# A routed two-layer feed-forward: the second layer's bias leaves TensorE for GpSimd, and its result alternates between two PSUM banks

## What is computed

```
t = to_tokens(x)                                # 2048 tokens x 192
gate_scores = ln(t) @ gate_w + gate_b           # 2048 x 6
topk_scores, topk_idx = top_k(gate_scores, 2)
topk_weights = softmax(topk_scores, axis=1)
hmid = gelu(einsum('nh,ehf->nef', ln(t), w1) + b1)    # 768 wide
expert_out = einsum('nef,efh->neh', hmid, w2) + b2    # 192 wide
sel = take_along_axis(expert_out, topk_idx[:, :, None], axis=1)
out = t + einsum('nk,nkh->nh', topk_weights, sel)
```

## Time and profile before

| what | value |
| --- | --- |
| three timed runs | 419.43, 415.05, 419.24 us; median 419.24 us |
| span of the profiled execution | 416.4 us; the page gives no other time of its own for it |
| TensorE busy | 349.8 us, 84% of the span |
| TensorE weight loads busy | 299.6 us, 72% |
| VectorE busy | 243.6 us, 59% |
| ScalarE busy | 182.3 us, 44% |
| GpSimd busy | 133.4 us, 32% |
| mean granted TensorE clock | 0.907 of 2.4 GHz |

### The profile page before, as it was taken

The page is one execution under the profiler, slowest core; times in us unless marked ns, Lnnn a source line. Parts: engine busy times, 40 slices in busy tenths (PEclk is TensorE's granted clock), DMA queues, the critical chain, the costliest instruction groups (busy, mean ns, idle before and its releaser), DMA issues.

```text
span 416.4 us, 10239 instructions
## 1 busy us (share of the span) xinstructions
PE 349.8 (84%) x2780; PEld 299.6 (72%) x2781; DVE 243.6 (59%) x961; ACT 182.3 (44%) x447; POOL 133.4 (32%) x163
## 2 busy tenths in 40 slices
PE   2668989889898889873089999999999999999625
PEld 0136877777777778662079999999999999999512
DVE  4443677777777777555235655555555656555246
ACT  1325767666666645430114434434344443444213
POOL 0000657766676773234101111122111221112100
PEclk9888999999999999955559999999999999999855
DMA  6422433323333310001301111111111111110066
GB/s 184 128 58 83 126 88 113 97 95 95 95 95 95 104 39 19 21 19 38 107 21 29 49 34 41 44 37 44 34 38 47 30 40 45 29 48 20 12 234 220
DMA packets 28053, 29.09 MB, mean 70 GB/s; under 512 B 5498, under 2 KB 24325, under 8 KB 28033
## 3 DMA queue, kind: packets, MB, share of 16 engines
q1 hardware_dynamic: 22498, 21.17, 17.9%
q0 software_dynamic: 3312, 6.33, 4.5%
q10 hardware_dynamic: 2222, 1.35, 1.2%
HBM read 20.00 MB, written 9.28 MB: 70 GB/s over the span
## 4 chain that ended last, share of the span: by engine, by line
PE 45%; DMA 3%; DVE 3%; SPq 1%; issue 1%; ACT 1%; POOLq 0%; DVEq 0%
PE bank L903 18%; PE up_ps L903 17%; PE up_ps L1107 7%; DVE prob L890 2%; DMA w2s<-made 1%; PE bank L1086 1%; PE bank L1087 1%; DMA routed<-xpad 1%; DMA made<-row,dest 1%; SPq L289 1%; DMA row<-routed 0%; SPq L290 0%; PE bank L1151 0%; SPq L385 0%; ACT pT L573 0%
## 5 line engine op out<-in xcount | busy, mean ns | idle before, releaser
L447 POOL DMA_INDIRECT made<-row,dest x37 | 36.4, 985 | 160.0 <-DVE row L862 160.0
L903 PE MATMUL bank<-w2s,split 128*128 x444 | 73.4, 315 | 1.4 <-DVE split L853 1.4
L903 PEld LDWEIGHTS bank<-w2s,split 128*128 128x128 f32 x444 | 65.7, 193 | 1.7 <-issue 1.6
L573 ACT ACTIVATE pT<-up_ps 128x768 f32<-128x768 f32 x37 | 30.1, 813 | 44.1 <-PE up_ps L903 44.1
L853 DVE TENSOR_TENSOR split<-up_ps,split 128x384 fp32r<-128x384 f32 x74 | 37.8, 553 | 15.3 <-ACT split L580 15.3
L422 POOL DMA_INDIRECT routed<-row,slot x32 | 32.9, 1027 | 39.8 <-issue 39.8
L903 PE MATMUL up_ps<-w1h,split 128*128 x148 | 42.5, 369 | 1.5 <-DVE split L848 1.5
L580 ACT ACTIVATE split<-up_ps 128x384 fp32r<-128x384 f32 x74 | 32.3, 488 | 18.7 <-PE up_ps L1107 18.7
L587 ACT ACTIVATE prob<-bank 128x192 f32<-128x192 f32 x37 | 12.3, 331 | 54.2 <-PE bank L903 54.2
L1107 PE MATMUL up_ps<-cst,pT 128*128 128x128 f32 x222 | 33.0, 286 | 0.5 <-ACT pT L573 0.5
L861 DVE COPY dest<-ring 128x1 int32 (+1 forms) x37 | 5.7, 154 | 47.2 <-ACT prob L587 47.2
(11 more groups left out here) (161 smaller groups left out, 766.7 us busy)
## 6 DMA issues: line engine op xcount, KB each, us to landing
row<-routed SPq DMA_DIRECT2D x37, 97.0 KB, 1.9
raw<-in_w SPq DMA_DIRECT2D x12, 288.0 KB, 3.6
w2s<-made SPq DMA_DIRECT2D x8, 384.0 KB, 7.2
raw<-in_w SPq DMA_DIRECT2D x6, 384.0 KB, 3.5
raw<-in_w SPq DMA_DIRECT2D x12, 192.0 KB, 3.4
arena<-in_coords SPq DMA_DIRECT2D x8, 256.0 KB, 3.4
xin<-in_x SPq DMA_DIRECT2D x16, 96.0 KB, 2.1
out<-arena SPq DMA_DIRECT2D x4, 192.0 KB, 4.0
```

Of the source, the lines that this page charges most:

```text
L447: pool.indirect_dma_start(out=made[:, :], out_offset=bass.IndirectOffsetOnAxis(ap=dest[par][:, :], axis=0), in_=yrow[par][:, 0:C], in_offs ...
L573: act.activation(hid.rearrange("p (n c) -> p n c", n=2), up_ps[:, 0:2, 0:HW_F], ACT.Gelu).then_inc(a_gelu, 1)
L903: return pe.matmul(o, a, b_, start=start, stop=stop)
```

## The change

Five things change together.

1. The thirteenth product of `down` goes, with `ones2`, `b2r`, the two small DMAs that filled b2r, the load of b2 to split and the two VectorE instructions that split it.
2. `b2all`, all 6 biases in f32 on every one of the 128 partitions, is loaded by one broadcasting DMA from SyncE's queue, at the end of its list for stage A.
3. GpSimd gets `add_b2`: it reads the expert's number into a register, waits for ylow_(b), and adds the bias to ylow in SBUF. VectorE's y_out(b) waits for that add (`g_b2`) and no longer for ScalarE.
4. down(b) writes bank[1] and bank[3] in turn (`bank_y`), and ylow has two buffers, so down(b) and ylow_(b) wait for y_out(b-2) and no longer for y_out(b-1).
5. VectorE's order in a block becomes lo(b), x_parts(b+2), y_out(b-1). The loops of ScalarE and VectorE are cut differently to fit.

```diff
+        b2all = sb("b2all", [P, E * C])
...
-        ones2 = sb("ones2", [2, P], f32r)
...
+        def bank_y(par):
+            return bank[1 + 2 * par]
...
-                sp.dma_start(b2r[k:k + 1, :].bitcast(f32), b2parts[k].bitcast(f32)).then_inc(s_rows, 16)
...
+            sp.dma_start(b2all[:, :], b2.rearrange("e c -> (e c)").partition_broadcast(P)).then_inc(s_b2, 16)
             sp.wait_ge(s_hot, NSTEP)
             sp.dma_start(c_all, table_d).then_inc(s_table, 16)
...
+            pool.wait_ge(v_tab, 12)
+            pool.wait_ge(s_b2, 16)
+
+            def add_b2(b, par):
+                e = pool.value_load(exp_i[0:1, bass.ds(b, 1)], min_val=0, max_val=E - 1)
+                pool.wait_ge(a_ylow, b + 1)
+                pool.tensor_tensor(ylow[par][:, :], ylow[par][:, :], b2all[:, bass.ds(e * C, C)], ALU.add).then_inc(g_b2, 1)
+
             def store_rows(b, par):
+                add_b2(b, par)
                 wait_apart(pool, v_yrow, b + 1)
...
-            def ylow_(b):
+            def ylow_(b, par):
                 act.wait_ge(p_dn, b + 1)
-                if not isinstance(b, int) or b >= 1:
-                    act.wait_ge(v_yrow, b)
-                act.activation(ylow[:, :], bank[1][:, C:2 * C], ACT.Copy).then_inc(a_ylow, 1)
+                if not isinstance(b, int) or b >= 2:
+                    act.wait_ge(v_yrow, b - 1)
+                act.activation(ylow[par][:, :], bank_y(par)[:, C:2 * C], ACT.Copy).then_inc(a_ylow, 1)
...
             def y_out(b, par, turn):
-                dve.wait_ge(a_ylow, b + 1)
+                dve.wait_ge(g_b2, b + 1)
...
-                dve.tensor_tensor(yrow[par][:, 0:C], bank[1][:, 0:C], ylow[:, :], ALU.add).then_inc(v_yrow, 1)
+                dve.tensor_tensor(yrow[par][:, 0:C], bank_y(par)[:, 0:C], ylow[par][:, :], ALU.add).then_inc(v_yrow, 1)
...
-                y_out(b, par, turn)
+                if not isinstance(b, int) or b >= 1:
+                    y_out(b - 1, 1 - par, turn)
...
-            def down(b, e):
-                if not isinstance(b, int) or b >= 1:
-                    pe.wait_ge(v_yrow, b)
+            def down(b, par, e):
+                if not isinstance(b, int) or b >= 2:
+                    pe.wait_ge(v_yrow, b - 1)
...
-                mm(bank[1][:, 0:C], ones2[:, :], b2r[:, bass.ds(e * C, C)], start=False, stop=True).then_inc(p_dn, 1)
+                ins.then_inc(p_dn, 1)
```

More of the change, by code:

```diff
@@ L28 @@
 NSTEP = L * L // RC
-NLOAD = 10
+NLOAD = 9
 _at = {}
@@ L91, in program @@
         w2s = sb("w2s", [P, E * FT, 2 * C], f32r)
-        b2r = sb("b2r", [2, E * C], f32r)
+        b2all = sb("b2all", [P, E * C])
         raw1 = [sb(f"raw1_{n}", [P, F]) for n in range(2)]
@@ L116, in program @@
         ytok = sb("ytok", [P, NT, C])
-        b1raw, b2raw = raw1[1][0:E, :], raw2[1][0:E, 0, :]
+        b1raw = raw1[1][0:E, :]
         b1parts = [w1l[0:E, E - 1 - k, :] for k in range(2)]
-        b2parts = [w1l[0:E, E - 3, k * C:(k + 1) * C] for k in range(2)]
         xin = sb("xin", [CH, 2, P])
@@ L167, in program @@
         xh, xl, xm, xe = (split[:, 2 * F + n * P:2 * F + (n + 1) * P] for n in range(4))
-        ylow = prob[0][:, 6:9, :].rearrange("p a b -> p (a b)")
+        ylow = [prob[n][:, 6:9, :].rearrange("p a b -> p (a b)") for n in range(2)]
         ring = sb("ring", [P, NBLK], i32)
@@ L234, in program @@
         v_lo, v_bxh, v_bx, v_ring, v_yrow = (sem(n) for n in ("v_lo", "v_bxh", "v_bx", "v_ring", "v_yrow"))
+        s_b2, g_b2 = sem("s_b2"), sem("g_b2")
         s_made = [sem("s_made0"), sem("s_made1")]
@@ L428, in _ @@
                 slot_(s // 2, s % 2)
-            pool.wait_ge(s_rows, 16 * 4)
+            pool.wait_ge(s_rows, 16 * 2)
             with pool.Fori(LOOP_A, NCH // 2) as i:
@@ L467, in _ @@
             act.dma_start(b1raw, b1).then_inc(s_bload, 16)
-            act.dma_start(b2raw, b2).then_inc(s_bload, 16)
             def bias_out(n):
@@ L581, in hi, with blk @@
                                    ACT.Copy).then_inc(a_hi, 1)
-            def ylow_(b):
+            def ylow_(b, par):
                 act.wait_ge(p_dn, b + 1)
-                if not isinstance(b, int) or b >= 1:
-                    act.wait_ge(v_yrow, b)
-                act.activation(ylow[:, :], bank[1][:, C:2 * C], ACT.Copy).then_inc(a_ylow, 1)
-            gelu(0)
[L590 to L598, removed]
+                if not isinstance(b, int) or b >= 2:
+                    act.wait_ge(v_yrow, b - 1)
+                act.activation(ylow[par][:, :], bank_y(par)[:, C:2 * C], ACT.Copy).then_inc(a_ylow, 1)
+            def blk(b, par):
+                hi(b)
+                if not isinstance(b, int) or b + 1 < NBLK:
+                    gelu(b + 1)
+                ylow_(b, par)
+            gelu(0)
+            blk(0, 0)
+            blk(1, 1)
+            with act.Fori(1, (NBLK - 1) // 2) as i:
+                blk(2 * i, 0)
+                blk(2 * i + 1, 1)
+            for b in range((NBLK - 1) // 2 * 2, NBLK):
+                blk(b, b % 2)
             for b in range(B):
@@ L607, in _ @@
             dve.memset(ones[:, :], 1.0)
-            dve.memset(ones2[:, :].bitcast(f32), 1.0)
             dve.memset(oT[CH:CH + 1, :, :], 1.0)
@@ L775, in _ @@
             dve.wait_ge(s_bload, 16 * NLOAD)
-            for raw, parts in ((b1raw, b1parts), (b2raw, b2parts)):
-                ins = dve.tensor_copy(parts[0], raw)
-            ins.then_inc(s_parts, 1)
+            dve.tensor_copy(b1parts[0], b1raw).then_inc(s_parts, 1)
             dve.wait_ge(s_parts, 1)
-            for raw, parts in ((b1raw, b1parts), (b2raw, b2parts)):
-                ins = dve.tensor_tensor(parts[1], raw, parts[0].bitcast(f32), ALU.subtract)
-            ins.then_inc(s_parts, 1)
+            dve.tensor_tensor(b1parts[1], b1raw, b1parts[0].bitcast(f32), ALU.subtract).then_inc(s_parts, 1)
             for s in range(0, 2 * LOOP_A):
@@ L870, in blk @@
                     x_parts(b + 2, par)
-                y_out(b, par, turn)
+                if not isinstance(b, int) or b >= 1:
+                    y_out(b - 1, 1 - par, turn)
             blk(0, 0, 0)
             blk(1, 1, 0)
-            with dve.Fori(1, (NBLK - 2) // 2) as i:
-                blk(2 * i, 0, i)
+            blk(2, 0, 0)
+            with dve.Fori(1, (NBLK - 3) // 2) as i:
                 blk(2 * i + 1, 1, i)
-            for b in range((NBLK - 2) // 2 * 2, NBLK):
-                blk(b, b % 2, b // 2)
+                blk(2 * i + 2, 0, i)
+            for b in range((NBLK - 3) // 2 * 2 + 1, NBLK):
+                blk(b, b % 2, (b - 1) // 2)
+            y_out(NBLK - 1, (NBLK - 1) % 2, (NBLK - 1) // 2)
             def gated(t, k):
@@ L1117, in down @@
                         pe.wait_ge(v_lo, 2 * b + f // 3 + 1)
-                    mm(bank[1][:, 0:2 * C], hTh[:, f, :], w2f[:, bass.ds(at2 + f * 2 * C, 2 * C)], start=f == 0, stop=False)
-                    mm(bank[1][:, 0:C], hTl[:, f, :], w2f[:, bass.ds(at2 + f * 2 * C, C)], start=False, stop=False)
-                mm(bank[1][:, 0:C], ones2[:, :], b2r[:, bass.ds(e * C, C)], start=False, stop=True).then_inc(p_dn, 1)
+                    mm(bank_y(par)[:, 0:2 * C], hTh[:, f, :], w2f[:, bass.ds(at2 + f * 2 * C, 2 * C)], start=f == 0, stop=False)
+                    ins = mm(bank_y(par)[:, 0:C], hTl[:, f, :], w2f[:, bass.ds(at2 + f * 2 * C, C)], start=False,
+                             stop=f == FT - 1)
+                ins.then_inc(p_dn, 1)
             pe.wait_ge(v_tab, 12)
             pe.wait_ge(s_lo, NCH)
-            pe.wait_ge(s_rows, 16 * 4)
+            pe.wait_ge(s_rows, 16 * 2)
             e_now = expert(0)
@@ L1135, in blk @@
                     rows_in(b + 2, par, done)
-                down(b, expert(b))
+                down(b, par, expert(b))
             blk(0, 0, 2, 32)
```

## The result

The changed kernel takes 400.52 us in the median of 4 runs (399.35 to 401.14), against 419.34 for the kernel before (4 runs, 415.05 to 420.27): 18.8 us less. The ratio is 0.9574, 95% interval 0.9519 to 0.9629. The forecast was 406.3 us, with a range down to 402.0.

What follows compares the result with a forecast made beforehand. TensorE was taken to bound stage B. Removing the bias product in 36 blocks (-13.3 us) and the last block's net cost (+0.4) summed to -12.9 us, from 419.24 to 406.3 us; range 402 to 411.5 us.

Steps and rivals of the forecast that it cites:

- The product that goes: TensorE, blocks 0 to 35: removing the bias product saves 0.37 us each, 13.3 us in all, bounds 5.4 and 15.8.
- Why the gaps go with it: TensorE's idle gaps of 0.16 and 0.10 us around the 2-row product's weight load are array drains and vanish with it.
- The new block, what else could be late: Stage B block of 4.38 us: ScalarE and VectorE steps keep room; the second bank brings nothing by itself.
- GpSimd's part: Add on GpSimd takes 0.61 us (0.47 to 1.41), covered in steady state; full ring 3.48 us, below 4.38.
- Rival 2: GpSimd's ring becomes the bound at 5.07 us a block, making the kernel slower, 432 us; chance 0.04.
- The last block: Uncovered add costs 0.8 us, the missing product gains some 0.43: net +0.4 us, between +0.15 and +1.8.
- I count all of this as 0: Ahead of stage B: loading b2all and dropping the early small DMAs and two splitting instructions changes the time by 0.
- The median of the runs stands 2.8 above that span: Whole kernel: 2.8 us added to the predicted span of 403.5 us gives the predicted median of 406.3 us.

Runs made afterwards that it cites:

- Experiments 3 and 4: Kernel before with the bias product made 128 rows high by zero rows: 407.09 us; kernel before with the 2-row product made twice: 421.29 us (one execution).
- experiment 2: Kernel before with the bias product kept, but two banks, two ylow buffers and y_out one block later: 419.87 us, ratio 1.0017.
- experiments 8 and 15: Changed kernel with three more GpSimd adds ahead of each real one: 415.23 us; with two more: 402.84 us; one execution each.
- experiment 7: Changed kernel without GpSimd's add and its register read, b2 missing from the output: 399.38 us.
- experiments 2 and 12: Kernel before with two banks and later y_out: 419.87 us; kernel before with 34 unread TensorE products ahead of stage B's first block: 411.89 us.
- experiments 13 and 14: Changed kernel with 34 unread TensorE products ahead of the first block: with unused early b2 work put back, 401.96 us; without it, 400.28 us.
- 9 and 10: Changed kernel unaltered, run again: 398.39 us, ratio 0.9638; kernel before with only the bias product removed, run again: 397.67 us, ratio 0.9565.
- the two warm kernels: Changed kernel and kernel before, each with 34 unread TensorE products ahead of stage B's first block: 397.07 and 411.89 us.
- The repeat: Changed kernel unaltered, run again beside the kernel before on another occasion: 398.39 us against 414.28, ratio 0.9638.

## Why the forecast was wrong

Two steps failed. One term was mis-sized: the 0.37 us for the bias product, "and I take that", measured 0.424 us. That alone would have given 404.3 us, still within the range. The other is a term that the sum did not have: it was set against one profiled span, 416.4 us, without a price for what TensorE's clock had done in that execution. The clock came back late at the start of stage B, which cost 2.1 us there that the profile after does not have, and fell once more in the last block, 1.5 us.

**The product that goes: mis-sized, low.** "so a pair costs 0.29 us; the last pair is done with its slot at 287.46" held: the six pairs from 282.47 to hidT's start at 284.23 now take 0.293 us each. What the 0.37 us left out stands behind hidT's start. Before, the transposes' first weight load came after idle time, and they took 0.63 us until `up`:

```profile
288.46 0.60 PE L903 MATMUL up_ps<-w1h,split 128*128 x2
```

(287.83 to 288.46); now their first weight loads are made beneath the last w2s products, and it is 0.58 (284.23 to 284.81). So the product cost 0.424 us (4.750 - 4.326), close to the 0.44 that the weight path gave as the upper bound: 36 x 0.424 = 15.3 us in place of 13.3. The time between starts counts a gap's near side only; the groups of weight loads had both.

**Why the gaps go with it: right.** Experiments 3 and 4 show that the gaps belong to the change of height and not to a thirteenth product. The page TensorEngine Tiling (Array Packing) of the Trainium skill, Key Properties, says that a change of tiling mode makes the array drain. The runs agree with that, at 0.31 us for there and back, if a product of 2 rows is such a change; no row here shows the mode itself. That the clock's level stretched the gap had pointed the same way.

**The new block, what else could be late: right.** Nothing was; the block is 4.33 us and the second bank changes nothing (experiment 2).

**GpSimd's part: right, and on the safe side.** The add is 0.61 us as estimated. The register read was taken as exposed, and lies beside the DMA instruction. Rival 2's mechanism exists, but it takes four adds to reach it (experiments 8 and 15). The GPSIMD Engine Reference of the Trainium skill, Engine selection, would have the add on VectorE. No run does that; experiment 7, which leaves the add out altogether, suggests that it could gain at most the 0.8 us of the last block.

**The last block: the add right, the surroundings wrong.** +0.76 us for the add. But the step took the 3.35 us of the 12 products for granted. In that execution the granted clock fell to half from 390 to 392 us, and the copy came 6.05 us after hidT:

```profile
390.00:392.00 2.00, 2.00 (x9) 2.00 (x9) 0.00 (x0) 0.00 (x0) 0.15 (x1) 0.50 0.03 7
```

None of the 16 other profiles has this fall: the two that also keep one 2-row product (experiments 2 and 12) show 4.50 and 4.51 us. So it was a property of one execution, worth 1.5 us.

**"I count all of this as 0": probably wrong.** Over the 17 profiles stage B's first transpose stands at 209.6 us on average in the nine kernels that do the early work on b2 (207.4 to 212.3), at 207.8 in the eight that don't (205.2 to 209.6). Within each of the three occasions that have both kinds, those with the work start later on average, by 1.3 to 2.4 us. The medians of experiments 13 and 14 differ by 1.7 us in the same direction. But the medians of 9 and 10 point the other way, and single starts overlap. So 1 to 2 us is likely, not shown. It is also no part of the 18.1 us between the two profiles, where stage B began 0.45 us later after the change.

**"The median of the runs stands 2.8 above that span": one execution taken for the kernel.** A run's time is 1.8 us above its span (400.11 and 398.3), so the other 1.0 of the 2.8 is scatter between executions. The profiled execution of before had the shortest stage A but one of the nine profiles with the early work, and the late return of the clock. The first transpose to the second hidT took 13.75 us there and 11.31 after, 2.1 more than the 0.37 by which the two warm kernels differ. Of the 13 profiles without the 34 products, six have this short form (11.3 to 11.6) and seven the long one (12.7 to 13.8). All six have two banks, only one with two banks is long. TensorE's instructions are the same until the clock returns, and no run shows a way by which two banks could bring it back earlier. Experiment 2 has two banks and the short form, yet its median is not below the kernel before's. Whether the link is chance stays open.

In sum, 15.3 + 0.3 - 0.8 = 14.8 us is what the change does by means that the runs show. Of the 18.1 us between the two profiles the rest is the clock, 2.1 us in the first blocks and 1.5 in the last, less 0.3 at both ends. The 18.8 us between the first medians are 4 us more than 14.8 as well; which part of them is the clock and which the start of stage B no run separates. The repeat gave 15.9 us, the warm pair 14.8. That the first comparison fell below 402 us was thus in part chance; the mis-sized product was not.

## What to carry to other kernels

Before moving a small product off TensorE, look at its height: a product of 2 rows among products of 128 cost 0.42 us, of which 0.31 went with zero rows added to fill the height. Price a removed instruction by the idle and busy time of the weight loads on both sides of it as well (here 0.44 us, against 0.42 measured), not by the starts of its neighbours alone (0.37). A small extra step on an idle engine costs only where no block covers it; count the ring through that engine (scatter, read, add, next result) against the block's length. And when a profile's clock changes level within the stretch that is compared, take the difference of two kernels from a version in which it does not.

## What was not expected of the hardware

- Work that nobody needs, on a TensorE that would wait 11 us, gained 1.3 and 2.4 us in the medians, little beside the scatter. In the profiles the granted clock was then full at the first block, and the first transpose to the second hidT was 1.8 and 3.8 us shorter.
- Two kernels with the same instructions until stage B differ by up to 4.8 us in its start (207.49 and 212.29), and the same kernel before had medians of 414.28 and 418.85 us on the same chip on different occasions.
- A second 2-row product directly behind the first costs 0.12 us, as much as one of 128 rows; only the passage between heights costs more, 0.31 us there and back.
